# Another order of key blocks, diagonal maxima and background tasks in a causal attention and gated feed-forward kernel

## What is computed

```python
xn = layernorm(x)
q, k, v = split(xn @ W_attn + b_attn)        # 16 heads of 16 channels
q, k = rope(q), rope(k)                      # the angle depends on the head, not on the token
att = softmax(causal(q @ k.T / 4))           # 1024 x 1024 for each head
s = (att @ v) @ W_proj + b_proj
g = silu( (silu(xn @ wg.T) * (xn @ wu.T)) @ wd.T )   # hidden width 768, 8-bit integer weights times 1/127
out = x + s * g
```

## Time and profile before

| what | value |
|---|---|
| device time, three runs | 1334.45 us median (1330.52 to 1334.53) |
| the profiled execution | 1334.66 us; its span 1332.8 us, 1.9 us lie around it |
| mean granted PE clock | 0.978 of 2.4 GHz |
| PE, ACT, DVE, POOL busy | 96%, 71%, 74%, 52% of the span |
| first scores of the first batch | 77.55 us |
| slot 0 of batch 4 (batches count from 0) | 697.38 us; from batch 1 on one batch takes 155.66 us |
| last `values` | 1317.29 us |

### The profile page before, as it was taken

How to read it: one execution, slowest core, us unless ns; L and a number is a source line. 1 busy time by engine, 2 the same in 40 slices (tenths; PEclk the granted TensorE clock), 3 DMA queues, 4 the chain that set the end, 5 groups by cost and what they waited for, 6 DMA issues and landing times.

```text
span 1332.8 us, 30434 instructions
## 1 busy us (share of the span) xinstructions
PE 1278.7 (96%) x11399; PEld 572.6 (43%) x11399; DVE 986.3 (74%) x1930; ACT 948.3 (71%) x2090; POOL 687.3 (52%) x850
## 2 busy tenths in 40 slices
PE   2899999999999999999999999999999999999996
PEld 1334433445344443544444453444435454444433
DVE  6788787877877877787777778778777878767721
ACT  2147777786777777777777867777777777778673
POOL 4116443584437734475545844377344755455642
PEclk9679999999999999999999999999999999999988
DMA  2630022302041020400213020410204002120001
GB/s 84 182 81 2 20 62 63 99 1 71 27 128 34 9 89 18 128 18 23 76 57 105 1 73 26 127 34 4 94 17 128 18 17 82 54 75 2 23 11 48
DMA packets 56854, 73.70 MB, mean 55 GB/s; under 512 B 9026, under 2 KB 35074, under 8 KB 56708
## 3 DMA queue, kind: packets, MB, share of 16 engines
q1 hardware_dynamic: 56420, 71.38, 17.8%
q10 hardware_dynamic: 288, 0.39, 0.1%
HBM read 46.01 MB, written 25.17 MB: 53 GB/s over the span
## 4 chain that ended last, share of the span: by engine, by line
PE 90%; DVE 4%; ACT 3%; DMA 1%; POOL 1%; issue 1%; ACTq 0%; POOLq 0%; SPq 0%; DVEq 0%
PE ring L741 30%; PE acc L733 22%; PE st L679 16%; PE ring L703 8%; PE ring L828 4%; PE ring L714 3%; PE ring L803 3%; DVE mx_a L1036 2%; ACT pexp L908 2%; PE ring L837 1%; PE ring L818 1%; PE ring L751 1%; DVE mx_b L1036 1%; DMA xn<-in_x 1%; DMA k_st<-parts_scratch 0%
## 5 line engine op out<-in xcount | busy, mean ns | idle before, releaser
L908 ACT ACTIVATE pexp<-st 128x512 f32<-128x512 f32 (+3 forms) x1536 | 659.0, 490 | 108.7 <-PE st L679 101.9
L1036 DVE TENSOR_REDUCE mx_a<-ring 128x1 f32<-128x512 f32 (+3 forms) x896 | 529.6, 646 | 76.0 <-PE ring L714 42.5
L1256 POOL TENSOR_SCALAR_AFFINE_SELECT pexp<-pexp 128x512 f32<-128x512 f32 x256 | 163.3, 638 | 541.8 <-ACT pexp L908 541.0
L733 PE MATMUL acc<-pexp,v_pad 128*17 128x512 f32 (+3 forms) x3072 | 324.7, 495 | 5.1 <-POOL pexp L1256 4.2
L679 PE MATMUL st<-q_st,k_st 50*128 50x512 f16 (+3 forms) x1536 | 282.5, 334 | 8.8 <-ACT pexp L908 8.3
L703 PE MATMUL ring<-k_st,q_st 48*128 48x512 f16 (+3 forms) x1536 | 264.2, 332 | 8.0 <-DMA k_st<-parts_scratch 5.0
L1036 DVE TENSOR_REDUCE mx_b<-ring 128x1 f32<-128x384 f32 (+3 forms) x384 | 212.2, 595 | 66.0 <-PE ring L714 65.7
L679 PEld LDWEIGHTS st<-q_st,k_st 50*128 50x128 f16 x1536 | 82.9, 93 | 375.2 <-ACT pexp L908 276.4
L1287 POOL TENSOR_TENSOR hf<-ga,ups 128x512 f32<-128x512 f32 x96 | 122.1, 1272 | 14.6 <-issue 10.4
L714 PE MATMUL ring<-tri,ident 64*128 64x128 bf16 (+2 forms) x1536 | 121.9, 219 | 0.0
L1296 POOL TENSOR_TENSOR hT<-hf,hT 128x512 f16<-128x512 f32 x96 | 111.3, 1160 | 3.8
(11 more groups left out here) (113 smaller groups left out, 1521.2 us busy)
## 6 DMA issues: line engine op xcount, KB each, us to landing
parts_scratch<-parts SPq DMA_DIRECT2D x32, 512.0 KB, 2.8
q_st<-parts_scratch SPq DMA_DIRECT2D x192, 64.0 KB, 2.2
k_st<-parts_scratch SPq DMA_DIRECT2D x186, 64.0 KB, 2.2
xn<-in_x SPq DMA_DIRECT2D x8, 1024.0 KB, 5.9
xo<-in_x SPq DMA_DIRECT2D x32, 256.0 KB, 2.8
out<-xo SPq DMA_DIRECT2D x32, 256.0 KB, 2.2
q_st<-mT SPq DMA_DIRECT2D x128, 4.0 KB
pexp<-in_w_attn SPq DMA_DIRECT2D x1, 768.0 KB, 4.7
```

The lines of the kernel that those rows point to most:

```text
L733: mm = nc.tensor.matmul(acc[32 * j:32 * j + D + 1, CH - w:CH], v_pad[:, kb, GH * g + j, :], pexp[:, GH * (n % NSET) + j, 0:w], start=n in ...
L908: nc.scalar.activation(pexp[:, GH * (n % NSET) + j, 0:w], st[:, (GH * n + j) % NST, 0:w], ACT.Exp, scale=1.0 / (QK_SCALE * np.sqrt(D))).th ...
L1036: nc.vector.reduce_max(dst, ring[:, b, 0:len(heads) * w].rearrange("p (s w) -> p s w", w=w), AX.X)\
L1256: nc.gpsimd.affine_select(out=t, in_=t, compare_op=ALU.is_ge, fill=0.0, base=0, pattern=[[0, GH], [1, P]], channel_multiplier=-1).then_inc ...
```

## The change

The order of the 12 steps in `BLOCKS`, the order of the diagonal pieces, the steps with maxima off the diagonal, and the two task tables are replaced. The number of instructions of each kind and their shapes stay. Two small edits belong to it: the product of `UPU` on POOL waits for `h_low` of the tile two before instead of `h_high`, and the epilogue's mask is conditional (the last step is (1, 6), which is on the diagonal).

```diff
@@ -24,8 +24,8 @@
 NEG = -3.0e38
 
 
-BLOCKS = [(0, 0), (0, 1), (0, 2), (0, 3), (1, 0), (1, 1), (1, 2), (1, 3), (1, 4), (1, 5), (1, 6), (1, 7)]
-DIAG_ORDER = (0, 1, 2, 3, 4, 5, 6, 7, 8, 9, 10, 11)
+BLOCKS = [(0, 0), (0, 2), (0, 3), (0, 1), (1, 4), (1, 5), (1, 0), (1, 1), (1, 2), (1, 7), (1, 3), (1, 6)]
+DIAG_ORDER = (11, 0, 9, 7, 5, 10, 8, 6, 1, 4, 2, 3)
 
 
 def width(n):
@@ -51,7 +51,7 @@
     return 6 + (s - 8) // 2, CH, P * (3 + (s - 8) // 2), ((s - 8) % 2,)
 
 
-FULL = (0, 2, 3, 4, 6, 7, 8, 9)
+FULL = (1, 2, 4, 6, 7, 8, 10, 11)
 
 
 def full_item(s):
@@ -61,50 +61,49 @@
 
 
 TASKS = {
-    0: [("DN", 1, 2)],
-    1: [("UPG", 0, 0), ("FT", 0)],
-    2: [("UPG", 0, 1), ("FT", 1)],
-    3: [("FP", 0)],
-    4: [("DN", 1, 3), ("XC", 0)],
-    5: [("LNS", 0), ("LNS", 1), ("UPU", 0, 0)],
-    6: [("FP", 1)],
-    7: [("V", 0, 1), ("LNS", 2), ("LNS", 3)],
-    8: [("UPU", 0, 1)],
-    9: [("MT", 1), ("YT", 3, 1)],
-    10: [("FT", 2)],
-    11: [("UPG", 0, 2), ("LNR",), ("UPU", 0, 2)],
-    12: [("V", 1, 0), ("V", 1, 1), ("YT", 0, 0)],
-    13: [("LNA", 2), ("UPG", 0, 3), ("UPG", 0, 4)],
-    14: [("FT", 3)],
-    15: [("LNA", 4), ("UPU", 0, 3)],
-    16: [("LNA", 0), ("LNA", 7)],
-    17: [("UPG", 0, 5), ("UPU", 0, 4)],
-    18: [("XC", 1), ("UPU", 0, 5)],
-    19: [("YT", 1, 0), ("LNA", 1)],
-    20: [("UPG", 1, 0)],
-    21: [("MT", 2), ("YT", 0, 1), ("LNA", 3), ("LNA", 5)],
-    22: [("TX", 1, 0), ("TX", 0, 0), ("FP", 2), ("LNA", 6)],
-    23: [("TX", 1, 1), ("TX", 0, 1), ("DN", 0, 0)],
-    24: [("DN", 0, 1)],
-    25: [("DN", 0, 2)],
-    26: [("QK", 0, 1, 0), ("QK", 0, 0, 1), ("QK", 0, 1, 1), ("QK", 0, 0, 0), ("DN", 0, 3)],
-    27: [("UPG", 1, 1), ("UPU", 1, 0)],
-    28: [("UPU", 1, 1), ("YT", 1, 1)],
-    29: [("FP", 3)],
-    30: [("UPG", 1, 2)],
-    31: [("QK", 1, 0, 0)],
-    32: [("UPG", 1, 3)],
-    33: [("MT", 3), ("YT", 2, 0)],
-    34: [("UPU", 1, 2)],
-    35: [("V", 0, 0)],
-    37: [("QK", 1, 1, 0)],
-    38: [("YT", 2, 1)],
-    39: [("UPG", 1, 4), ("UPU", 1, 3)],
-    41: [("UPG", 1, 5), ("UPU", 1, 4)],
+    0: [("UPG", 0, 0), ("UPG", 0, 1), ("DN", 1, 2)],
+    1: [("V", 0, 1), ("DN", 1, 3), ("FT", 0)],
+    2: [("UPU", 0, 0)],
+    4: [("UPG", 0, 2), ("UPU", 0, 1)],
+    5: [("LNS", 0), ("LNS", 1), ("FT", 1), ("XC", 1), ("LNS", 2), ("FP", 0)],
+    6: [("UPU", 0, 2)],
+    7: [("FP", 1), ("LNS", 3)],
+    8: [("V", 1, 0)],
+    9: [("MT", 1)],
+    10: [("UPG", 0, 3), ("LNR",)],
+    12: [("V", 1, 1), ("LNA", 2), ("YT", 3, 1)],
+    13: [("UPG", 0, 4), ("LNA", 1)],
+    14: [("UPU", 0, 3), ("FT", 2)],
+    15: [("YT", 0, 0)],
+    16: [("UPU", 0, 4)],
+    17: [("UPG", 0, 5), ("FT", 3)],
+    18: [("XC", 0), ("LNA", 5), ("UPU", 0, 5)],
+    19: [("YT", 0, 1)],
+    20: [("UPG", 1, 0), ("UPG", 1, 1)],
+    21: [("LNA", 0), ("LNA", 3), ("MT", 2), ("YT", 1, 0)],
+    22: [("LNA", 7), ("TX", 0, 0), ("TX", 1, 0), ("DN", 0, 0)],
+    23: [("LNA", 4), ("QK", 0, 1, 0), ("DN", 0, 1), ("LNA", 6)],
+    24: [("TX", 1, 1), ("TX", 0, 1), ("DN", 0, 2)],
+    25: [("QK", 0, 1, 1), ("QK", 0, 0, 1), ("QK", 0, 0, 0)],
+    26: [("V", 0, 0)],
+    27: [("DN", 0, 3)],
+    28: [("UPU", 1, 0)],
+    29: [("QK", 1, 1, 0)],
+    30: [("UPU", 1, 1)],
+    31: [("FP", 2)],
+    32: [("UPG", 1, 2)],
+    33: [("MT", 3)],
+    34: [("UPU", 1, 2), ("YT", 2, 0)],
+    35: [("UPG", 1, 3)],
+    36: [("UPU", 1, 3), ("YT", 1, 1)],
+    37: [("QK", 1, 0, 0)],
+    38: [("FP", 3)],
+    40: [("UPG", 1, 4), ("UPU", 1, 4)],
+    41: [("QK", 1, 0, 1), ("UPG", 1, 5)],
     42: [("UPU", 1, 5)],
-    43: [("QK", 1, 0, 1)],
-    44: [("QK", 1, 1, 1)],
-    45: [("MT", 0), ("YT", 3, 0)],
+    43: [("YT", 3, 0)],
+    44: [("QK", 1, 1, 1), ("YT", 2, 1)],
+    45: [("MT", 0)],
     46: [("DN", 1, 0)],
     47: [("DN", 1, 1)],
 }
@@ -119,21 +118,21 @@
 EPI = [("YT", 3, 1), ("FT", 2), ("FT", 3), ("FP", 2), ("FP", 3)]
 END_FROM = 28
 END_TASKS = {
-    28: [("YT", 1, 1), ("UPU", 1, 1)],
-    29: [("FP", 3)],
+    28: [("UPU", 1, 0), ("UPU", 1, 1)],
     30: [("UPG", 1, 2), ("UPU", 1, 2)],
-    31: [("UPG", 1, 3), ("UPU", 1, 3)],
-    32: [("UPG", 1, 4), ("UPU", 1, 4)],
-    33: [("MT", 3), ("YT", 2, 0), ("UPG", 1, 5)],
-    34: [("UPU", 1, 5)],
-    38: [("YT", 2, 1), ("DN", 1, 0)],
-    39: [("DN", 1, 1)],
-    40: [("DN", 1, 2, "end")],
-    41: [("DN", 1, 3, "end")],
-    42: [("YT", 3, 0)],
-    43: [("FT", 0, "end"), ("FT", 1, "end")],
-    44: [("FP", 0, "end")],
+    31: [("FP", 2)],
+    32: [("UPG", 1, 3), ("UPU", 1, 3)],
+    33: [("MT", 3), ("UPG", 1, 4)],
+    34: [("YT", 2, 0), ("UPU", 1, 4)],
+    35: [("UPG", 1, 5), ("UPU", 1, 5)],
+    36: [("YT", 1, 1)],
+    38: [("FP", 3)],
+    41: [("DN", 1, 0)],
+    42: [("YT", 3, 0), ("DN", 1, 1)],
+    43: [("FT", 0, "end"), ("FT", 1, "end"), ("DN", 1, 2, "end")],
+    44: [("YT", 2, 1), ("FP", 0, "end")],
     45: [("FP", 1, "end")],
+    46: [("DN", 1, 3, "end")],
 }
 
 
@@ -1283,7 +1282,7 @@
                     wait_done(pool, kind, i, ("UPG", c, m))
                     wait_done(pool, kind, i, t)
 
-                    wait(pool, h_high, k - 2)
+                    wait(pool, h_low, k - 2)
                     nc.gpsimd.tensor_tensor(hf[:, u, :], ga[:, u, :], ups[:, u, :], ALU.mult).then_inc(h_full, 1)
                 if t[0] == "HI":
                     _, c, m = t
@@ -1378,7 +1377,8 @@
                             task(kind, i, t)
 
             def epilogue():
-                mask(B - 1, GROUPS - 1, STEPS - 1)
+                if is_diag(STEPS - 1):
+                    mask(B - 1, GROUPS - 1, STEPS - 1)
 
             run(pool, body, prologue, epilogue)
 
```

## The result

| what | before | changed |
|---|---|---|
| device time, median | 1333.8 us (1330.52 to 1334.53, 4 runs) | 1342.49 us (1337.91 to 1342.87, 4 runs) |
| the profiled execution | 1334.66, span 1332.8 | 1337.91, span 1336.1 |
| first scores | 77.55 | 76.06 |
| first batch, from slot 0 to slot 0 | 151.76 | 147.43 |
| batch 4, the same way | 155.66 | 156.92 |

The ratio is 1.0062, 95% interval 1.0034 to 1.009: slower by 0.6%. Forecast 1339, range 1323 to 1350.

A forecast was written before the change was run, and what follows sets the result against it. The prediction took PE to bound the kernel, at full clock in the middle batches. From the profiled 1334.66 us it added 6.7 (six middle batches), -2.5 (first batch and prologue) and 0 (last batch): 1339, range 1323 to 1350.

The forecast's parts named there:

- Part 1: Middle batches: PE's waits for exponentials sum to 2.31 us instead of 3.32, so 1.0 saved a batch.
- Part 2: Slot 12, batches 1 to 7: rows of maxima of group 1 arrive late, PE waits 2.1 us each.
- the collision: SP, slot 9: FP 1's store and load queue ahead of group 1's maxima; forecast 2.1 us wait at slot 12.
- Part 3: Prologue and first batch: less DVE work before slot 0, PE tasks moved into slots 0 to 11; -2.5 us.
- Part 4: Last batch: waits in slots 25, 29 and 12 against relief at masks and the end; sum 0, bounds -4 and +4.
- the relief at the masks: Last batch: fewer UPU crowd POOL, so a mask wait of up to 2.7 us near 1280 goes.
- A: Slot 12: the rows of maxima are there in time, no wait of 2.1 in seven batches; 1324 us, chance 0.25.
- B: Slots 3, 5, 10, 15, 19, 24: DVE and the four ring banks limit, 1.6 us a batch; 1350, chance 0.17.
- C: Slot 12, seven batches: the wait drops PE's clock, 3.4 us lost each, +24; 1363 us, chance 0.04.

The follow-up runs named there:

- e2_mt_first: Changed kernel, but SP serves MT before FP where both fall into one half slot (slots 9, 33): 1332.2 us, ratio 0.9985 to the kernel before.
- e1_repeat: Changed kernel again with no edit, for a second profile: median 1339.8 us, ratio 1.0045 to the kernel before; its profiled execution took 1343.48.
- e6_both_moves: Changed kernel with FP 1 in slot 11 instead of 7, and FP 2 and UPG(1, 2) swapped between slots 31 and 32: 1328.63 us, ratio 0.9956.
- e8_short_pool: Changed kernel with POOL's FP_X pass of FP 2 adding only 64 of 512 columns, so output is incomplete: 1337.21 us, one time.
- e3_orders: Kernel before with the new orders of blocks, diagonal pieces and off-diagonal maxima, old task tables except V(0, 1) moved from slot 7 to 1: 1365.79 us, ratio 1.0241.
- e7_before_fp1_7: Kernel before with only FP 1 moved from slot 6 to slot 7: 1341.97 us, ratio 1.0061.
- e9_longer_wait: Changed kernel, but SP waits for FP 1's load to land before issuing the maxima of group 1: 1369.47 us, ratio 1.0276.

## Why the prediction was right, and where it was not

**Part 1** (-1.0 a middle batch) was right. Slots 3 and 39 have 0.44 each above their work (forecast 0.43), the three slots that n = 10 holds up 0.21 (0.20), the two that n = 3 holds up 0.10 and 0.11 (0.15), and slots 10 and 11 together 0.53 in e2_mt_first, where nothing else stands there (0.55). Sum 2.25, forecast 2.31.

**Part 2** (+2.1) was right in mechanism, moment and size: slot 6 to slot 12 takes 19.48, forecast 19.5. But 2.1 is not all wait for the DMA. PE stood 1.21 at `MT` 1 and then 0.88 at slot 12. The chain ran beside both, and the first wait cost nothing, since PE would have stood that time later: in the last batch of e1_repeat `MT` 1 hardly waited, and slot 6 to slot 12 took 19.93 all the same. The last of several waits sets the length of a stretch; what stands before it is hidden in it.

**The step that failed** in the middle batches is the sentence that `MT` comes behind a slot without off-diagonal maxima and waits 0. I had looked at what DVE has to do before `MT`, not at what POOL does at that moment. `MT` 1 waits 1.21, hidden while the collision is there and laid bare by e2_mt_first, and `MT` 3 waits 0.57 in the open (slot 33 takes 2.92, and 2.35 in e6_both_moves and e8_short_pool). So a middle batch is +1.26 and not +1.1: -1.1 for the exponentials, +2.1, +0.6 for `MT` 3, and 0.3 less that I can't place. The six of them, batches 1 to 6, gave +7.2 for the forecast 6.7; batch 1 alone gave only 0.3, as it took 156.67 before. That 1.0 stands in its slot 0 (3.97, and 2.96 in batch 2), whose maxima waited 0.87 for DVE's `mx_a`; the changed kernel has no such wait.

**Part 3** (-2.5) was mis-sized: -5.8 in the first profile, beyond its bound of -5. By how much hangs on the execution. Seven profiles here have this prologue and the same work in the first batch, and the start of slot 0 of batch 1, 223.3 to 226.1, lies 3.2 to 6.0 ahead of the 229.31 of before. From slot 2 on they agree (138.7, before 143.1); what varies is the first scores, 75.0 to 78.3, and slots 0 and 1, 8.7 to 9.6 together. So the forecast was too small against all seven, and the 1.5 that the first scores came earlier in the first profile is within that variation: that DVE's shorter reductions in the prologue gave it is not shown. Slots 0 and 1 take 8.74 in the first profile for the 8.68 of before, with a `V` and a gate product more in them, 1.36 + 0.97: 2.3. I had these. The clock goes with them. PE before, in the stretches around its first scores:

```profile
77.00:79.00 2.00, 1.16 (x4) 0.23 (x3) 2.00 (x5) 0.83 (x2) 0.00 (x0) 0.50 0.36 105
79.00:82.00 3.00, 2.77 (x18) 1.13 (x18) 2.14 (x5) 1.79 (x5) 0.30 (x1) 0.50 0.51 141
82.00:86.00 4.00, 4.00 (x17) 0.69 (x14) 2.40 (x4) 1.67 (x4) 0.77 (x2) 0.50 0.75 216
```

and changed:

```profile
77.00:79.00 2.00, 2.00 (x10) 0.75 (x7) 1.49 (x3) 0.76 (x2) 0.00 (x0) 0.50 0.58 150
79.00:82.00 3.00, 2.47 (x17) 0.86 (x15) 1.88 (x3) 2.42 (x6) 0.09 (x1) 0.97 0.49 124
```

The kernel comes out of the prologue at 1.2 GHz. Before, PE stood 1.07 near 78 and the clock came back at 86.3; changed, PE had no pause there and it came back at 79.2. In the other profiles with the new prologue it came back between 80.8 and 83.4, the last of these in e3_orders, which has no pause either; in e7_before_fp1_7, with the old prologue, at 86.4. So it comes back earlier in each of the new ones, and the pause is not all of it. Another 2 us or so are in slots 12 to 47, which I had not looked at: in the first batch the `FP` of the old table fall away, and slot 29 (n = 5) then stood 1.1 above its work; in the new table it holds a `QK` and stands at 0. How much of the gain is order and how much table stays open, since e3_orders mixes it with the waits of its old table.

**Part 4** (0) was off by +1.9, inside its bounds. Slots 25 and 29 wait 0.94 and 1.10 (forecast 1.0 and 1.1), the end gives -1.5 (-1.1). What did not come is the relief at the masks, and that term was a misreading: the 2.7 of the earlier trace rows is not near 1280 but at the very end, in slot 47, and near 1280 no wait for a mask was over 0.42. In the changed kernel PE waits for masks 1.37 in slot 37, 1.31 in slot 40 and 1.66 behind slot 47, again 4.3 in all. Two waits of before, and the one of slot 40:

```profile
1279.82 0.39 PE L679 MATMUL st<-q_st,k_st 50*128 50x512 f16 x1 [0.53 <-ACT pexp L908]
...
1315.47 1.06 PE L733 MATMUL acc<-pexp,v_pad 128*17 128x256 f32 x8 [2.73 <-POOL pexp L1256]
```

```profile
1293.67 0.89 PE L732 MATMUL acc<-pexp,v_pad 128*17 128x384 f32 x8 [1.31 <-POOL pexp L1255]
```

**The sum** has luck in it. 1338.9 is 1.0 above the profiled execution because the gain of part 3 was forecast 3.3 too small, and the middle batches 0.5 and the last one 1.9 too short.

**The rivals.** A (rows in time, 1324) fell; e2_mt_first and e6_both_moves show what it would have given, 1332 and 1329. B (DVE and the banks) came in another form: not a full DVE, but a DVE held up by POOL. C (the clock) I had given 0.04, since I expected a wait at slot 12 "shorter than the one before the fall". That rested on the same misreading: the fall of the earlier trace rows at 1281 had no wait of 2.7 before it, but several of up to 0.53. In the middle batches the clock stayed at 1.00 all the same, with the wait cut in two by `MT` 1. In the last batch of the second profile it did not, and e9_longer_wait makes it fall in every batch, at 1369. That this is near the 1363 of rival C is chance: C had 3.4 a fall for the clock alone, and e9_longer_wait shows 2.4 of longer wait and 1.4 for the clock. The rule of the Trainium skill, "TensorE: Matmul & The Clock Gate", section "HAM oscillation — how this bites in real kernels", that a DMA wait in each round of a loop brings the low clock back each time, agrees with e9_longer_wait (0.52 behind the wait of batch 4, a low stretch behind each of the seven). In the middle batches of the changed kernel the DMA wait of each round is short, and their clock is 1.00, so a wait in each round is not enough by itself.

The median of 1342.5 lies 3.5 above the forecast and 4.6 above the profiled execution. The two profiles of the changed kernel differ by the clock in the last batch, and that is the likely place of this difference too. The mean granted clock of all ten executions fits: 0.983 to 0.985 in the five of 1337.1 to 1339.9 us, 0.977 to 0.981 in the five of 1342.3 to 1343.7.

## What to carry to other kernels

When a hand-made table moves a task, follow its parts on every queue, those of the engine that only issues DMAs first: a store, a load into the same buffer and an urgent little transfer in one half slot made a chain of 19 us out of queues for which nobody had waited, and serving the urgent one first gave back 7.6. Look also at what runs beside an instruction, not only at what stands before it: here 0.6 of the 1.3 us a batch came from short DVE work that fell under a long POOL pass, and two tasks of neighbouring slots changing places cured it. And price a long wait of PE together with the slow clock behind it: 2.4 us more of waiting cost 3.8.

## What the runs showed of the hardware

DVE's short instructions that read and write SBUF alone are held up until a POOL pass that already runs is through: a `mx_p` of 32 columns took 1.16 beside a pass of 1.28 and 0.20 beside one of 0.33, and the long one ended within 0.1 us of the pass. DVE's reductions out of PSUM keep their 0.6 beside the same passes. The Trainium skill has this on "SBUF — State Buffer", section "Who interferes with whom": the two engines share a port pair, which one instruction holds to its end while the other waits. The trace agrees, with these numbers, and shows the price: 0.6 to 1.2 us of PE for 0.2 us of DVE's work.

The clock of TensorE fell from 2.4 to 1.2 GHz behind a single wait of 3.3 us without a weight load (e1_repeat; 2.4 without a matmul) and behind seven of about 4 (e9_longer_wait; 3.0 to 3.9 without a matmul), and not behind the same wait in two pieces of 1.4 and 1.75 with almost 6 us of work between them. Slot 12 at the low level took 5.24 in place of 3.61. But a long wait is not the only thing ahead of a fall: in the last batch the clock also fell at 1294.3 behind a wait of 1.31 for a mask (the changed kernel's first profile), and at 1281 behind waits of at most 0.53, several within 6 us (the kernel before).

With the same program it fell at slot 12 of the last batch in one profiled execution and not in the other. Whether `MT` waits there hung on which of DVE and POOL started first, within 0.1 us: `mx_p` and the POOL pass began at 1198.11 and 1198.10 in the first profile, and `mx_p` took 1.31; both began at 1197.85 in the second, and it took 0.21.
